# Folding the value weights inside tile 0, splitting the setup's waits, and norming rows ahead of the residual in a one-core attention and MoE kernel

## The reference

```python
B, Lq, Q_DIM = 16, 64, 256            # 1024 query rows; 1601 context rows per batch, all f32
H, HD, KVC, QC, R = 16, 128, 64, 96, 64
kv_c = kv @ W_kvc                     # context -> 64
q_c = layernorm(x) @ W_dq             # rows -> 96
q_nope = q_c @ W_uq ; q_rope = rope(q_c @ W_qr)
k_nope = kv_c @ W_uk; k_rope = rope(kv_c @ W_kr)
v = kv_c @ W_uv                       # 16 heads of 128
scores = (q_nope . k_nope + q_rope . k_rope) / sqrt(192)
scores = where(seg - 8 <= key <= seg, scores, -1e30)
out = softmax(scores) @ v @ W_o       # 2048 -> 256
x = x + out
...
x = x + self_attention(layernorm(x))
x = x + moe(layernorm(x))             # 8 experts, 2 chosen, 2 shared
```

## Time and profile before

| | |
|---|---|
| median of 3 runs | 528.61 us (528.29 to 529.51) |
| profiled execution | 530.75 us, of which the profile's span is 528.9 us |
| PE busy | 504.2 us (95%) |
| DVE busy | 253.0 us (48%) |
| ACT busy | 186.3 us (35%) |
| POOL busy | 60.5 us (11%) |
| DMA | 82.08 MB moved, mean 155 GB/s |
| chain that ended last | PE 83%, DVE 7%, issue 5%, ACT 2%, DMA 2% |

### The profile page before, as it was taken

One profiled execution on the slowest core, in us unless ns is written; L12 is line 12 of the kernel. 1 busy time (PEld: TensorE's weight loads), 2 busy tenths in 40 slices (PEclk: granted clock), 3 DMA queues, 4 the chain that ended last, 5 costly groups with the idle time before them and its releaser, 6 DMA issues.

```text
span 528.9 us, 10582 instructions
## 1 busy us (share of the span) xinstructions
PE 504.2 (95%) x3876; PEld 364.0 (69%) x3876; DVE 253.0 (48%) x549; ACT 186.3 (35%) x533; POOL 60.5 (11%) x71
## 2 busy tenths in 40 slices
PE   8989999999999979998899999899999999999997
PEld 6566776767767768886688887455555555556886
DVE  3765765866856657989644221222222222222235
ACT  2266566556567524444331111221121121121110
POOL 2000000000000012223103520000000000000650
PEclk9898999999999989999999999999999999999999
DMA  9700000000892005900162235488778778762231
GB/s 301 293 20 4 18 21 0 20 20 0 292 422 100 2 5 193 403 4 0 22 280 90 79 108 213 148 300 299 269 285 307 270 276 316 266 244 71 84 119 47
DMA packets 24459, 82.08 MB, mean 155 GB/s; under 512 B 2881, under 2 KB 16513, under 8 KB 20322
## 3 DMA queue, kind: packets, MB, share of 16 engines
q1 hardware_dynamic: 21536, 75.93, 39.5%
q0 software_dynamic: 1536, 4.20, 2.5%
q10 hardware_dynamic: 1346, 1.38, 0.8%
HBM read 73.11 MB, written 8.39 MB: 154 GB/s over the span
## 4 chain that ended last, share of the span: by engine, by line
PE 83%; DVE 7%; issue 5%; ACT 2%; DMA 2%; DVEq 1%; SPq 0%; POOL 0%; ACTq 0%; POOLq 0%
PE ps L1790 17%; PE ps L1703 12%; PE ps L1307 10%; PE ps L1814 9%; PE ps L1715 6%; PE ps L1386 5%; PE ps L1336 5%; PE ps L1355 5%; PE ps L1470 3%; PE ps L1374 2%; DMA w_routed<-in_w_qr 2%; PE ps L1328 1%; ACT w_routed L1086 1%; PE ps L1480 1%; PE ps L1659 1%
## 5 line engine op out<-in xcount | busy, mean ns | idle before, releaser
L1790 PE MATMUL ps<-w_routed,xnT 128*64 x320 | 93.8, 436 | 1.6 <-DVE x_sb L956 1.6
L1703 PE MATMUL ps<-xT_all,w_shared 128*128 128x256 f32 x320 | 75.7, 380 | 0.0
L1790 PEld LDWEIGHTS ps<-w_routed,xnT 128*64 128x64 f32 x320 | 42.0, 137 | 38.4 <-issue 27.2
L1703 PEld LDWEIGHTS ps<-xT_all,w_shared 128*128 128x128 f32 x320 | 60.3, 190 | 8.4 <-issue 0.4
L1086 ACT ACTIVATE w_routed<-ps,neg_top 128x128 f32<-128x128 f32 x128 | 45.1, 379 | 19.4 <-DVE neg_top L626 19.4
L1307 PEld LDWEIGHTS ps<-consts_a,w_routed 128*128 128x128 f32 x336 | 38.2, 144 | 19.6 <-issue 16.1
L1307 PE MATMUL ps<-consts_a,w_routed 128*128 128x128 f32 x336 | 46.4, 282 | 5.2 <-DVE w_routed L614 1.8
L1814 PE MATMUL ps<-w_routed,hidT 128*64 x200 | 47.4, 384 | 0.0
L1790 PE MATMUL ps<-x_up,xnT 128*64 128x384 f32 (+1 forms) x160 | 46.9, 436 | 0.0
L1790 PE MATMUL ps<-w_shared,xnT 128*64 128x384 f32 (+1 forms) x160 | 46.9, 436 | 0.0
L1249 ACT ACTIVATE sil<-ps 128x256 f32<-128x256 f32 x40 | 15.3, 384 | 84.7 <-PE ps L1703 60.6
(11 more groups left out here) (180 smaller groups left out, 877.0 us busy)
## 6 DMA issues: line engine op xcount, KB each, us to landing
w_routed<-in_w_routed SPq DMA_DIRECT2D x8, 1920.0 KB, 14.5
x_up<-in_w_routed SPq DMA_DIRECT2D x10, 1280.0 KB, 6.0
w_shared<-in_w_routed SPq DMA_DIRECT2D x10, 1280.0 KB, 5.9
b_down<-in_w_routed SPq DMA_DIRECT2D x10, 640.0 KB
w_shared<-in_w_routed SPq DMA_DIRECT2D x10, 640.0 KB, 5.7
w_shared<-in_w_shared SPq DMA_DIRECT2D x1, 3840.0 KB, 12.1
w_shared<-in_w_uvo SPq DMA_DIRECT2D x1, 2560.0 KB, 15.6
x_slots<-sil SPq DMA_DIRECT2D x16, 160.0 KB, 2.2
```

What stands on the lines that cost most here:

```text
L1703: last = pe.matmul(ps[:, UP_BANK[m], half_ * D:(half_ + 1) * D].rearrange("p (n t) -> p n t", n=2), w_shared[:, j, at:at + P], xT_all[:, i ...
L1790: last = pe.matmul(ps[rows, b, 0:hi - lo], xnT[:, k, rows], w, start=k == 0, stop=k == KT - 1)
```

## The change

1. The setup's block of 16 fold matmuls goes. A helper `fold_work(j, b)` makes a quarter of the fold (4 matmul calls) into one bank. PE does quarters 0 and 1 in `body(0)` where the other tiles have `project(i-1)`, into banks 4 and 5, and quarters 2 and 3 into the same banks behind both halves of q_T(1). DVE copies quarters 0 and 1 out, ahead of `divided(0, 1)`; ACT copies 2 and 3, behind `qt_hi_out(1)`. PE waits for the first two copies before quarter 2, and for the third before values(0,0), which writes bank 4.
2. w_qr gets a semaphore of its own, awaited ahead of y_rope(0); seg gets its own, awaited by DVE alone. PE's absorb_k and xT(0) wait for less.
3. `normed(i+2)` stands in `body(i)` behind `front_qt(i+1)` and ahead of `residual(i-1)`, in place of `normed(i+1)` at the head; `normed(1)` comes ahead of `body(0)`. The count of `rstd_ready` that it waits for is that of the same tile as before.

```diff
@@ sync @@
-            sp.dma_start(w_q[:, 1], dram["w_qr"]).then_inc(wk_in, 16)
+            sp.dma_start(w_q[:, 1], dram["w_qr"]).then_inc(wr_q_in, 16)
...
-            sp.wait_ge(absorb_m, 1)
+            sp.wait_ge(absorb_m, 4)
@@ vector, body @@
             def body(i, link_, behind, more):
-                normed(i + 1, (2, 3)[i] if isinstance(i, int) and i < 2 else 2 * i, xn, xT_ps, xn_ready, i + 1)
                 maxima(i, 0)
...
                 front_rotated(i + 1)
+                if not behind:
+                    for j in range(2):
+                        dve.wait_ge(absorb_m_ps, j + 1)
+                        dve.tensor_copy(w_m[:, 2 * j:2 * j + 2, :].rearrange("p j d -> p (j d)"), ps[:, 4 + j, :]).then_inc(absorb_m, 1)
                 divided(i, 1, link_)
                 front_qt(i + 1)
+                if more:
+                    normed(i + 2, 3 if isinstance(i, int) and i == 0 else 2 * i + 2, xn, xT_ps, xn_ready, i + 2)
                 if behind:
                     residual(i - 1, link_)
@@ vector, setup @@
-            dve.wait_ge(const_in, 16 * 2)
+            dve.wait_ge(const_in, 16)
+            dve.wait_ge(seg_in, 16)
...
             dve.wait_ge(x_in, 16)
+            normed(1, 2, xn, xT_ps, xn_ready, 1)
             body(0, link, False, True)
@@ scalar @@
-            act.dma_start(seg_i[:], dram["seg"]).then_inc(const_in, 16)
+            act.dma_start(seg_i[:], dram["seg"]).then_inc(seg_in, 16)
...
                 qt_hi_out(i + 1)
+                if not behind:
+                    for j in range(2, 4):
+                        act.wait_ge(absorb_m_ps, j + 1)
+                        act.copy(w_m[:, 2 * j:2 * j + 2, :].rearrange("p j d -> p (j d)"), ps[:, 2 + j, :]).then_inc(absorb_m, 1)
                 ut_out(i, 0)
...
             lat_out(0)
-            act.wait_ge(absorb_m_ps, 1)
-            act.copy(w_m[:].rearrange("p j d -> p (j d)"), ps[:, 4:8, :].rearrange("p b n -> p (b n)")).then_inc(absorb_m, 1)
             k_out(0)
@@ tensor @@
+            def fold_work(j, b):
+                for h in range(2):
+                    for p in range(2):
+                        head = 4 * j + 2 * p + h
+                        last = pe.matmul(ps[KVC * p:KVC * (p + 1), b, h * D:(h + 1) * D], w_uv[:, head, :], w_o[:, head, :],
+                                         start=True, stop=True)
+                return last
...
                 if behind:
                     project(i - 1)
+                else:
+                    pe.wait_ge(wv_in, 16)
+                    pe.wait_ge(pt_done, 1)
+                    for j in range(2):
+                        fold_work(j, 4 + j).then_inc(absorb_m_ps, 1)
                 k_T(i + 1)
                 q_T(i + 1, 0, qt_lo_ps)
                 q_T(i + 1, 1, qt_hi_ps)
+                if not behind:
+                    pe.wait_ge(absorb_m, 2)
+                    for j in range(2):
+                        fold_work(2 + j, 4 + j).then_inc(absorb_m_ps, 1)
+                    pe.wait_ge(absorb_m, 3)
                 values(i, 0)
@@ tensor, setup @@
-            pe.wait_ge(wk_in, 16 * 3)
+            pe.wait_ge(wk_in, 16 * 2)
...
-            pe.wait_ge(const_in, 16 * 2)
+            pe.wait_ge(const_in, 16)
...
             y_lat(0)
+            pe.wait_ge(wr_q_in, 16)
             y_rope(0)
-            pe.wait_ge(wv_in, 16)
-            for j in range(NP_ // 2):
...
-            last.then_inc(absorb_m_ps, 1)
...
-            pe.wait_ge(absorb_m, 1)
             pe.wait_ge(win_ready, 1)
             body(0, False)
+            pe.wait_ge(absorb_m, 4)
             body(1, True)
```

More of the change, by code:

```diff
@@ L278, in build @@
         b_dn_in = [sem(f"b_dn_in{q}") for q in range(2)]
-        names = """wu_in const_in x0_in x_in wk_in wv_in wo_in aw_in ctx_in win_ready dve_step pool_step
+        names = """wu_in wr_q_in seg_in const_in x0_in x_in wk_in wv_in wo_in aw_in ctx_in win_ready dve_step pool_step
             absorb_q_ps absorb_q absorb_k_ps absorb_k absorb_m_ps absorb_m
@@ L286, in build @@
         S = {n: sem(n) for n in names}
-        (wu_in, const_in, x0_in, x_in, wk_in, wv_in, wo_in, aw_in, ctx_in, win_ready, dve_step, pool_step,
+        (wu_in, wr_q_in, seg_in, const_in, x0_in, x_in, wk_in, wv_in, wo_in, aw_in, ctx_in, win_ready, dve_step, pool_step,
          absorb_q_ps, absorb_q, absorb_k_ps, absorb_k, absorb_m_ps, absorb_m,
@@ L1249, in gated @@
                 act.activation(sil_ring[m % 2], ps[:, UP_BANK[m], 0:D], ACT.Silu).then_inc(up_sil, 1)
-            act.wait_ge(absorb_m, 1)
+            act.wait_ge(absorb_m, 4)
             act.wait_ge(zeroed, 16 * ZC)
```

## The result

The changed kernel takes 523.09 us in the median of 4 runs (522.49 to 525.13), against 529.06 us (528.29 to 529.66, 4 runs) for the kernel before. The ratio is 0.9895, 95% interval 0.9863 to 0.9926: faster by about 5.5 us by the ratio (5.97 between the medians). Forecast were 524.2 and a range of 521.0 to 526.9.

A forecast was written before the change was run, and what follows sets the result against it. The prediction took TensorE's chain of waits to bound nearly the whole span. Its terms, -5.6 - 0.3 + 0.1 + 1.4 = -4.4 us, took the 528.6 median to 524.2, range 521.0 to 526.9.

The forecast's parts named there:

- Part 1: Loop tiles' ends: norm ahead of the residual closes TensorE's hole before xT, -5.6 us (bounds -5.9 to -4.6).
- Part 2: Setup: with waits split by transfer, kv(0) waits for the second context load until 13.1; y_rope(0) ends 0.2 us earlier, near 20.1.
- rival A: Setup: the clock doesn't fall at 11 us, y_rope(0) ends at 17.6, total -7.1 us, 521.5; chance 0.18.
- Part 3: Setup without the fold: VectorE's chain from y_rope(0) still bounds xT(1), at 27.05, so only -0.3 us.
- Part 4: Fold inside tile 0: first half free in a wait, second half +1.8 us, offset by expected full clock; net +0.1 us.
- Part 5: Start of tile 0: clock expected low after the setup's longer holes, costing +1.4 us, between 0 and 3.4.

The follow-up runs named there:

- fold in the hole: Changed kernel with two of four fold parts moved into the setup's hole, around k_T(0), their ScalarE copies behind the key copy: 521.22 us, ratio 0.9835 against before.
- hole filled: Changed kernel plus eight matmuls that nothing reads, six ahead of k_T(0) and two ahead of q_T(0): 523.06 us, ratio 0.9882 against before.
- the far operations later: Changed kernel with VectorE's four far-flag instructions moved from ahead of the first query copy to behind tile 1's norm: 523.1 us, ratio 0.9863 against before.

## Why the prediction came out as it did

The time lay in the range, 1.1 us below the forecast. Part of that closeness is luck: the steps fared differently.

**Part 1, the norm: mechanism right, term too small.** -5.6 forecast; 6.27 in the five stretches and 0.15 in the next (21.29 to 21.14), so -6.4. The term 19.08 for a full stretch took the last transposes' modelled end (start plus 1.09) as the end of TensorE's work. When work follows at once, it follows 0.93 behind that start (81.37 to 82.30). This is 0.16 in each of five tiles. TensorE's loop branch cost nothing, and neither did the later residual. The reason for the hole was told incompletely, though. The norm stood not only behind the residual but also behind VectorE's own loop branch: the earlier trace rows have 0.60 "issue" ahead of L576. At the last boundary of before there is no branch, since body 6 stands outside VectorE's loop:

```profile
146.62 0.41 DVE L576 TENSOR_SCALAR xn<-x_sb,mv,rstd 128x256 f32<-128x256 f32 x1
147.17 0.43 PE L1307 MATMUL ps<-consts_a,xn 128*128 128x128 f32 x2 [0.67 <-DVE xn L576]
```

There the norm follows the residual without idle time and TensorE waits 0.67 in place of 1.14. So about 0.45 us at each of the three boundaries inside the loop, some 1.4 of the 6.3, was the price of the branch. The new place of the norm avoids both; no run moves it ahead of the branch alone.

**Part 2, the split: the wait right, the clock not.** The context load did become the bound, at 13.33 (13.1 forecast). But y_rope(0) ended at 17.9 and not at 20.1, by rival A's mechanism: the clock didn't fall. Whose doing it was is not settled. With the split the clock was high throughout in four profiles (after, the changed kernel again, fold in the hole, hole filled) and low for some time in five; without it, low in all five. The four are those in which the absorb matmuls began at 6.9; in the five low ones with the split they began at 7.6 to 8.0. Before began at 6.86 and 6.7 and fell all the same, but with a hole of 1 us ahead of absorb_k (0.99 and 1.04). So an early start without that hole goes with the high clock. That is what the profiles have in common and not a test of it, and the length of a hole alone doesn't decide: the four waited 1.06 to 1.25 us ahead of kv(0) and stayed at the full clock. TensorE's queue is the same up to y_rope(0) in all nine profiles with the split, and in five of them the clock fell, at 12.9 to 13.7. The Trainium skill (TensorE: Matmul & The Clock Gate, "Part 1: The HAM clock gate") says that the point where the clock first rises differs from run to run of the same kernel. It says so of the rise at the start; these profiles show that the fall varies as well.

**Part 3: the chain right, its start not.** What left TensorE's queue in the setup didn't shorten the stretch from the end of the y blocks to xT(1), since VectorE's chain bounds the start of tile 0: it was 7.1 before and 7.3 to 7.4 after. xT(1) came 2.07 earlier in place of 0.3 because that chain began earlier. With the fold still in the setup an early end of the y blocks couldn't have been used in full: its weights land at 19.5 to 19.8, and in the profile after the y blocks end at 17.9. So in such an execution the move is worth something; a fold from 19.7 to 23.3 would put xT(1) near 26.7 in place of 25.28, an estimate that no run shows, since the clock was low in the one execution that was to show it (norm and split).

**Part 4: right against the profile it started from, wrong against the kernel.** Forecast for tile 0 was +0.1, seen +0.23 (18.95 to 19.18). But the sum set 1.8 us of fold against 1.7 us of low clock that only some executions pay. Where they don't, tile 0 takes 17.34 without the fold and 19.17 with it: +1.8. That the term looked right against the profile is luck. The cover that I named for the second half is a low that isn't always there. I had the alternative and placed it on the wrong side, as a risk of the changed kernel (+1.8 if the clock fell all the same).

**Part 5: mechanism right, size wrong.** The clock did fall in the hole, but recovered as tile 0 began, or within 0.3 us of it, in five of the six profiles with that hole. In the sixth (the far operations later) it reached 1.5 us into the tile. +1.4 forecast; the hole filled shows 0.3 to 0.5 for a low that ends with the hole. Something I hadn't foreseen came at 186 us: 1.05 of the gain was given back from there to 240 us, with a longer low in that execution. Since the second profile of before has the longer low too, this belongs to the pair of executions compared and not to the change.

So the sum of the forecast, -4.4, held terms that missed in both directions: for the profiled spans -6.4 (norm) - 2.1 (xT(1) earlier) + 0.2 (tile 0) + 1.1 (up to the norm at 240 us) - 0.2 (behind it) = -7.4. The profile of before was moreover a slow one of its kind (530.75 us against a median of 529.06), with the low at 42, so the medians lie closer together than the two spans. By the ratios, 0.9873 for the norm alone and 0.9887 to 0.9895 for the whole change, the norm accounts for the whole gain. The split alone can't be told from zero. The fold costs 1.3 us alone, and on top of the norm (0.991 against 0.9873, whose intervals overlap) perhaps 2.

## What to carry to other kernels

An instruction that the next tile waits for belongs ahead of one that nobody waits for soon; check its inputs, its target and what the displaced one releases; here each hole at a tile's end closed at no cost. Look at the engine's loop branch too: it stands between the last instruction of one pass and the first of the next. Work that moves off one engine's queue pays nothing if another engine's chain spans the same stretch, and it costs its length where it lands, unless it lands in a wait; the half that replaced a wait here was free, and putting the other half into the wait that its own removal had opened gave the lowest ratio (0.9835). A profile is one execution: before a stretch of low clock is used as cover for added work, a second profile should show it too, and a kernel that lacks it should be looked for.

## What the runs showed of the hardware

The same kernel's executions differ by the number and the length of TensorE's lows, and the time follows: 529.0 us in the median at a mean granted clock of 0.994 and 531.7 at 0.987. A hole of 1.06 to 1.25 us ahead of kv(0) left the clock full in four profiles. The lows inside the kernel last 3.4 or 6.8 us in these profiles. The one at 42 us is in none of the nine profiles in which the first half of the fold fills the wait ahead of q_T lo. It came behind holes of 1.79 and 0.26 us, and still came in only three of five profiles that had these holes.

A row's modelled end overstates a group of f32 transposes by 0.16 us against back-to-back starts (1.09 against 0.93 in the profile after); the distance of starts in a saturated stretch is the better measure.
